# A four-layer graph network: each layer's end as one pipelined block, sums that begin with x in them, small loads and flags beside the sums

## What is computed

```python
x = layernorm(x + L0(x))   # relational: h = relu(segsum(w1 * (x @ W[etype])[src]) + b1); the same again on h, + b2
x = layernorm(x + L1(x))   # graph: h = x @ W; dinv = rsqrt(max(in_deg, 1)); (h + segsum(w * h[src])) * dinv + bias
x = layernorm(x + L2(x))   # attention, 8 heads, twice: softmax over each node's edges, weighted sum; relu between
x = layernorm(x + L3(x))   # tensor product: messages from y[src], edge attributes and an MLP of the edge length
```

## Time and profile before

| what | us |
|---|---|
| median of 3 runs | 9986.03 (9984.52 to 9986.73) |
| the profiled execution's own time | 9983.22 |
| its span, first to last instruction | 9981.5 |
| TensorE busy | 7135.5 (71%) |
| GpSimd busy | 6743.2 (68%) |
| VectorE busy | 6099.3 (61%) |
| ScalarE busy | 3181.8 (32%) |

### The profile page before, as it was taken

How to read it: one execution, slowest core, us unless ns; L and a number is a source line. 1 busy time by engine, 2 the same in 40 slices (tenths; PEclk the granted TensorE clock), 3 DMA queues, 4 the chain that set the end, 5 groups by cost and what they waited for, 6 DMA issues and landing times. The chain is left out here.

```text
span 9981.5 us, 162608 instructions
## 1 busy us (share of the span) xinstructions
PE 7135.5 (71%) x35298; PEld 5014.6 (50%) x35298; DVE 6099.3 (61%) x20565; ACT 3181.8 (32%) x10805; POOL 6743.2 (68%) x7057
## 2 busy tenths in 40 slices
PE   3555554666677666669999857777477777499998
PEld 2222222333333333334444446566366666499998
DVE  8454553444434444446666557777577777699887
ACT  1222220000021000000000045555355555499997
POOL 1777776777734777757777467777377776277775
PEclk9999999999996555555555577877677777699999
DMA  3222222111143111111111122222122222211112
GB/s 89 79 83 84 80 82 78 53 53 53 53 180 136 53 53 53 53 48 53 53 53 53 33 59 60 60 60 60 38 60 60 60 60 52 68 53 52 53 52 45
DMA packets 290879, 638.27 MB, mean 64 GB/s; under 512 B 124766, under 2 KB 160609, under 8 KB 277745
## 3 DMA queue, kind: packets, MB, share of 16 engines
q0 software_dynamic: 224928, 422.56, 16.4%
q1 hardware_dynamic: 65392, 210.05, 6.1%
HBM read 481.27 MB, written 150.87 MB: 63 GB/s over the span
## 5 line engine op out<-in xcount | busy, mean ns | idle before, releaser
L806 POOL DMA_INDIRECT relsum_rows<-relation_table,tab_idx x1994 | 1894.7, 950 | 891.1 <-issue 532.1
L898 PE MATMUL relsum_sums<-relsum_hot,relsum_rows 128*128 128x128 f32 x3988 | 1575.4, 500 | 944.1 <-DMA relsum_rows<-relation_table,tab_idx 665.5
L898 PEld LDWEIGHTS relsum_sums<-relsum_hot,relsum_rows 128*128 128x128 f32 x3988 | 998.4, 312 | 1521.4 <-DMA relsum_rows<-relation_table,tab_idx 1500.6
L806 POOL DMA_INDIRECT conv_rows<-tensor_table,src_idx x1008 | 953.4, 946 | 502.8 <-issue 217.0
L806 POOL DMA_INDIRECT gcnsum_rows<-x_table,src_idx x997 | 945.0, 948 | 366.9 <-issue 231.3
L655 POOL DMA_INDIRECT records<-sort_recs,place_rows x968 | 987.5, 1020 | 295.1 <-issue 295.1
L884 DVE TENSOR_TENSOR rel_acc<-rel_acc,relsum_sums 128x128 f32 x1994 | 574.8, 288 | 992.9 <-PE relsum_sums L898 988.9
L806 POOL DMA_INDIRECT gat2sum_rows<-gat_table,src_idx x1008 | 955.2, 948 | 315.0 <-issue 223.4
L806 POOL DMA_INDIRECT gat1sum_rows<-gat_table,src_idx x1008 | 954.1, 947 | 314.9 <-issue 227.1
L865 DVE TENSOR_SCALAR relsum_hot<-iota_row,dst_rel,w 128x128 f32<-128x128 f32 x1994 | 712.0, 358 | 421.1 <-issue 419.9
L898 PE MATMUL gcnsum_sums<-gcnsum_hot,gcnsum_rows 128*128 128x128 f32 x1994 | 793.9, 502 | 0.0
(11 more groups left out here) (381 smaller groups left out, 14855.3 us busy)
## 6 DMA issues: line engine op xcount, KB each, us to landing
relation_table<-table_row SPq DMA_DIRECT2D x30, 2048.0 KB, 6.3
relation_table<-sort_space SPq DMA_DIRECT2D x40, 1024.0 KB, 5.7
relsum_rows<-relation_table,tab_idx POOLq DMA_INDIRECT x1994, 2.5
place_lo_wide<-lo_rows SPq DMA_DIRECT2D x121, 256.0 KB, 3.5
relation_table<-place_extra SPq DMA_DIRECT2D x20, 1024.0 KB, 5.8
gat1sum_rows<-gat_table,src_idx POOLq DMA_INDIRECT x1008, 2.5
gat2sum_rows<-gat_table,src_idx POOLq DMA_INDIRECT x1008, 2.5
conv_rows<-tensor_table,src_idx POOLq DMA_INDIRECT x1008
```

The source lines that it names most:

```text
L806: pool.indirect_dma_start(bufs[:, t % depth, :], None, table, bass.IndirectOffsetOnAxis(ap=idx[:, t:t + 1], axis=0)).then_inc(landed[t % l ...
L898: pe.matmul(bank[:, 0:P], rows[:, t % depth, :], hot[:, t % HOTS, :], start=True, stop=True).then_inc(s["multiplied"], 1)
```

## The change

- `load_sorted` is gone. `ReloadAndPrepare` runs beside the first relational sum: the records come in 16 pieces into three buffers; GpSimd waits before tile 0, 63, 126, ... for its piece's indices. SyncE then loads the second table's weights and 39 small tensors; TensorE turns x from tile 90 on (a quad of blocks every 4 tiles) and at tile 140 prepares the attention weights; ScalarE writes x turned, with the relational bias added, into the accumulator of the second sum.
- `second_table` gets the weights ready in SBUF and loads only its bias.
- The second relational sum and the graph sum do not clear their accumulator: it begins with x in it. In the graph sum TensorE first turns x (`pe_first`), VectorE then adds the graph bias to x, and only then the tiles start. The flags' groups come every 8 tiles instead of 16, and `crossing_runs` runs at tile 552 to 572.
- `finish_layer` takes the place of `per_node_block`, `normalize`, `project_nodes` and the stores for the first three layers. It works by units of 3 blocks and pairs of units: produce, add to x (or not), statistics, spread, root, shift, normalising by ScalarE, turning, product with the next layer's weights, copy, store of a pair. `finish_tensor_layer` does it for the last one.
- `between_attentions` divides by pairs and goes on with relu, product, copy and store per pair; GpSimd adds the second attention bias to x there.
- `first_scores` has moved into `attend`: its eight gathers are issued ahead of the others.
- Register loops around the nodes' work are unrolled. Three more scopes end with a barrier.

The core of the diff:

```diff
-def load_sorted(env, records):
-            sp.dma_start(rec[:, :, :], records.rearrange("(p q) k -> p q k", p=P)).then_inc(got, 16)
+class ReloadAndPrepare(Beside):
+    def sync(self, sp):
+        for c in range(PIECES):
+            if c >= 3:
+                sp.wait_ge(s["placed"], c - 2)
+                sp.wait_ge(s["weighed"], c - 2)
+            sp.dma_start(self.rec[:, c % 3, :, :], rows[:, c * PIECE:(c + 1) * PIECE, :]).then_inc(self.got[c % 3], 16)
...
+    def pool_at(self, pool, t):
+        if t % PIECE == 0:
+            pool.wait_ge(self.s["indexed"], t // PIECE + 1)
...
+        if t == self.WEIGHTS_AT:
+            pe.wait_ge(s["small_in"], 16 * self.small_loads)
...
+class GraphSum(Beside):
+    def pe_first(self, pe):
+        for q in self.quads():
+            if q:
+                pe.wait_ge(self.s["x_kept"], q)
+            for k, b in enumerate(range(4 * q, min(BLKS, 4 * q + 4))):
+                mm = pe.transpose(self.turn_ps[:, k * P:(k + 1) * P], self.env.x[:, b, :], self.env.ident[:, :])
+            mm.then_inc(self.s["x_turned"], 1)
...
+        dve.wait_ge(s["x_turned"], len(self.quads()))
+        x = self.env.x[:, 0:BLKS, :]
+        dve.tensor_tensor(x, x, over_rows(self.env.gcn_bias[:, :], BLKS), ALU.add)
+        dve.wait_ge(s["x_kept"], len(self.quads()))
...
+def finish_layer(env, tag, how, table=None, weights=None, width=None, scale=None, store_x=None):
+            for u in range(4):
+                make(u)
+            for u in range(UNITS):
+                if weights is not None:
+                    turn_x(u)
+                if u + 4 < UNITS:
+                    make(u + 4)
+                if weights is not None and u:
+                    apply(u - 1)
...
+            for g in range(PAIRS):
+                for u in (2 * g, 2 * g + 1):
+                    dve.wait_ge(s["made"], u + 1)
+                    if how.updates:
+                        how.update(dve, u, made[u % 4]).then_inc(s["freed"], 1)
+                        dve.drain()
+                    for k, b in enumerate(unit_blocks(u)):
+                        dve.bn_stats(env.stats[:, b, :], env.x[:, b, :] if how.updates else made[u % 4][:, k * P:(k + 1) * P])
+                dve.drain()
+                find_spread(dve, env, pair_blocks(g)).then_inc(s["measured"], 1)
+                if how.feeds and g + 2 < PAIRS:
+                    how.feed(dve, g + 2).then_inc(s["fed"], 1)
+                if g:
+                    dve.wait_ge(s["rooted"], g)
+                    find_shift(dve, env, pair_blocks(g - 1)).then_inc(s["shifted"], 1)
...
+            for g in range(PAIRS + 2):
+                if g < PAIRS:
+                    act.wait_ge(s["measured"], g + 1)
+                    act.activation(env.rstd[:, own], env.rstd[:, own], ACT.Sqrt, bias=env.eps[:, 0:1]).then_inc(s["rooted"], 1)
+                if 0 < g <= PAIRS:
+                    norm(g - 1)
...
+def between_attentions(env, acc, table):
+            floor_sums(dve, acc)
+            for g in range(PAIRS):
+                divide_sums(dve, acc, g).then_inc(s["divided"], 1)
...
+            pool.tensor_tensor(x, x, over_rows(env.gat_bias2[:, :], BLKS), ALU.add)
```

More of the change, by code:

```diff
@@ L723, in second_table @@
+def second_table(env, weights, table, hidden, bias):
     nc = env.nc
@@ L924, in per_node_block @@
-        block = ctx.enter_context(nc.Block())
+        made = [ps(f"made{j}", [P, 512], F32) for j in range(4)]
+        turn = [ps(f"turn{j}", [P, 512], F32) for j in range(2)]
+        out = [ps(f"out{j}", [P, 512], F32) for j in range(2)]
+        x_t = sb("x_t", [P, 2, UNIT * P], F32)
+        rows = sb("rows", [P, BLKS, width], F32) if weights is not None else None
+        how.memory(sb, ps, out[1])
+        s = {n: env.sig(f"{tag}_{n}").sem for n in (
+            "fed", "made", "freed", "measured", "rooted", "shifted", "normed", "turned", "kept", "applied", "taken",
+            "taken_dve", "stored")}
@@ L1066, in load_columns, with norm @@
-def load_columns(env, tag, pairs):
-    sig = env.sig("small_loaded")
-    with env.nc.Block() as block:
+            def norm(g):
+                act.wait_ge(s["shifted"], g + 1)
+                for u in (2 * g, 2 * g + 1):
+                    for k, b in enumerate(unit_blocks(u)):
+                        frm = env.x[:, b, :] if how.updates else made[u % 4][:, k * P:(k + 1) * P]
+                        last = act.activation(env.x[:, b, :], frm, ACT.Identity, bias=env.shift[:, b:b + 1],
+                                              scale=env.rstd[:, b:b + 1])
+                    last.then_inc(s["normed"], 1)
@@ L1566, in _ @@
             pe.sem_inc(s["turned"], PHASES)
+            pe.wait_ge(firsts["spread"].sem, firsts["spread"].at(1))
+            for j in range(FIRSTS):
+                mm = pe.matmul(firsts_ps[:, j * HEADS:(j + 1) * HEADS], first_wide[:, j, :, :].rearrange("p k h -> p (k h)"),
+                               env.head_mask[:, :], start=True, stop=True)
+            mm.then_inc(firsts["turned"].sem, 1)
             turn_scores(0, 0)
@@ L1602, in attend, with divide_sums, floor_sums @@
             landed[k].passed(16 * (GRPS // PHASES))
-def divide_sums(env, acc):
-    with env.nc.Block() as block:
+        for n, count in (("gathered", 16 * FIRSTS), ("spread", 1), ("turned", 1)):
+            firsts[n].passed(count)
+def divide_sums(dve, acc, pair):
+    cols = slice(2 * pair * UNIT * P, 2 * (pair + 1) * UNIT * P)
+    dve.reciprocal(acc[:, 1, cols], acc[:, 1, cols])
+    dve.drain()
+    return dve.tensor_tensor(acc[:, 0, cols], acc[:, 0, cols], acc[:, 1, cols], ALU.mult)
+def floor_sums(dve, acc):
+    dve.tensor_scalar(acc[:, 1, 0:NPAD], acc[:, 1, 0:NPAD], 1e-30, None, ALU.max)
+    dve.drain()
@@ new lines, in between_attentions @@
+def between_attentions(env, acc, table):
+    nc = env.nc
+    width = TABLE_WIDTH
+    pair_cols = 2 * UNIT * P
+    with ExitStack() as ctx:
+        sb, ps = stage_memory(nc, ctx, "between")
+        hidden = sb("hidden", [P, 2, pair_cols], F32)
+        rows = sb("rows", [P, BLKS, width], F32)
+        out = [ps(f"out{j}", [P, 512], F32) for j in range(4)]
+        s = {n: env.sig(f"between_{n}").sem for n in ("divided", "hidden", "applied", "taken", "stored")}
+        block = ctx.enter_context(nc.Block())
@@ new lines, in _ @@
+        @block.tensor
+        def _(pe):
+            for u in range(UNITS):
+                pe.wait_ge(s["hidden"], u // 2 + 1)
+                if u >= 4:
+                    pe.wait_ge(s["taken"], u - 3)
+                for k in range(UNIT):
+                    at = (u % 2 * UNIT + k) * P
+                    mm = pe.matmul(out[u % 4][:, k * width:(k + 1) * width], hidden[:, u // 2 % 2, at:at + P], env.gat_w[1][:, :],
+                                   start=True, stop=True)
+                mm.then_inc(s["applied"], 1)
@@ new lines, in finish_tensor_layer, with pair_blocks @@
+        sb, ps = stage_memory(nc, ctx, "tpout")
+        made = [ps(f"made{j}", [P, 512], F32) for j in range(4)]
+        turn = [ps(f"turn{j}", [P, 512], F32) for j in range(2)]
+        x_t = sb("x_t", [P, 4, UNIT * P], F32)
+        s = {n: env.sig(f"tpout_{n}").sem for n in ("turned", "kept", "made", "freed", "measured", "rooted", "shifted", "normed", "stored")}
+        block = ctx.enter_context(nc.Block())
+        def pair_blocks(g):
+            return slice(2 * g * UNIT, 2 * (g + 1) * UNIT)
```

1160 lines of the change are left out of this document (640 added, 520 removed).

## The result

The changed kernel takes 9755.95 us (median of 4 runs, 9751.77 to 9762.47) where the kernel before takes 9985.28 (4 runs, 9984.35 to 9986.73): a ratio of 0.9771, 95% interval 0.9754 to 0.9788. The profiled execution took 9753.1 us for a span of 9751.4, 230.1 us less than that of before. I had said 9759 and 227.2.

The account below looks back on a forecast made before the run. Gains were expected only at stage borders, 529 us where GpSimd has no gather to issue. Terms summed to 227.2 us off the profiled 9983.2, leaving 9756.0; with 2.8 for the median, 9759, range 9728 to 9802.

Parts of the forecast that it names:

- graph end: Border after the graph sum: 133.1 us to 60.1, gain 73.0 (60 to 80), VectorE slowest at 5.5 a pair.
- relational end: Border after the second relational sum: 55.2 us become 36.5, gain 18.7, bounds 8 and 24.
- graph sum's start: First gather to first tile of the graph sum: 23.9 us instead of 10.7, cost 13.2 (9 to 20).
- last end: Border after the convolution, to the kernel's end: 59.7 us become 47.0, gain 12.7 (8 to 16).
- attention end: Border between second attention and convolution: 129.0 us become 71.7, gain 57.3 (47 to 65).
- Records, second table: Reading before the first sum: gain 32.3 us (28 to 34); second table loading only its bias: 8.3 (5 to 9).
- Rival 3: Work beside the first relational sum isn't hidden: 20 to 60 us more, about 9800; chance 0.05.
- The ring: Relational end: a PSUM bank is free only once ScalarE has normalised it, so each pair takes 6.4 us.
- It is TensorE that sets this stage: its 1250 us start later: Graph sum: TensorE bounds it, so its later first tile delays the whole stage, cost 13.2 us.
- rival 1: Graph sum: the dense transposes at its start bring TensorE 2.4 GHz; 21 us less, 9738; chance 0.12.
- rival 2: Graph, attention and last ends: pipelines don't overlap, ScalarE's norms and hand-offs add 37 us, 9796; chance 0.17.
- Between: Border between the two attentions: 93.2 us become 55.1, gain 38.1 (28 to 42 if VectorE and GpSimd collide).

Follow-up runs that it names:

- the late folding: Changed kernel with the two flag-folding matmuls at tiles 976 and 984 instead of 560 and 568: 9753.08 us against 9752.79 (slower chip: 11429.56 against 11430.54).
- pairs first: Changed kernel with TensorE making the next pair's units before turning, VectorE's shift earlier, ScalarE normalising before the next root: 9719.45 us against 9752.79.
- The pieces: Changed kernel with GpSimd's add between the attentions cut into five, each beside a reciprocal: 9743.66 us against 9752.79.
- the second group: Runs on another chip than the slow first one; the changed kernel, unaltered, as yardstick there: 9752.79 us.

## Why the prediction was right, and where it was not

The forecast took the borders between stages, each wholly on the path, and sized what stays of each. That held nearly everywhere: but for the 3.6 us of the graph end's entry (below) no border's gain was lost elsewhere, and the long stages kept their time. Of the eight terms with bounds four lay within them; better than theirs were the relational end (25.1, bound 24), the graph sum's start (7.6 lost, bound 9) and the last end (17.0, bound 16), worse the attention end (46.4, bound 47). (By these same bounds the worst and the best sum are 164 and 261 us, which gives 9822 and 9725, not the 9814 and 9713 of the prediction.) Step by step:

*Records, second table.* As said. 16.2 us from the last scatter, 8.3 for the table, and 8.2 between the last gather's end and the request for the bias as before. Rival 3 is out.

*Relational end: a size.* The ring is 5.1 us a pair, not 6.4 (6 statistics in 1.3, six norms in 2.2, six turns in 2.0), and 30.0 in all.

*Graph sum: the step failed.* "It is TensorE that sets this stage: its 1250 us start later" did not hold: TensorE and the gathers are so close that a late start of TensorE can be made good within the stage. The late start (18.3 us, not 23.9: a quad takes 1.8, not 2.3) cost nothing at the sum's end, since the folding matmuls, which the change moves from the graph end into the sum, raise the clock for 31 us:

```profile
5047.59 0.80 PE L1097 MATMUL gcnsum_sums<-gcnsum_hot,gcnsum_rows 128*128 128x128 f32 x2
5048.31 1.88 PE L1408 MATMUL gcnsum_x_turn<-gcnsum_by_tile,head_sel 128*8 128x512 f32 x2
5049.98 0.63 PE L1096 MATMUL gcnsum_sums<-gcnsum_hot,ones 128*1 128x128 f32 x2
...
5052.26 0.38 PE L1096 MATMUL gcnsum_sums<-gcnsum_hot,ones 128*1 128x128 f32 x2
5052.57 0.49 PE L1097 MATMUL gcnsum_sums<-gcnsum_hot,gcnsum_rows 128*128 128x128 f32 x2
```

A matmul of 0.80 takes 0.49, a tile 0.73 instead of 1.24, and 17 us of lag become 4. From the first gather to the end 1261.6 us pass, and 1262.7 in the kernel before: of my cost of 13.2 nothing is left there. Up to the next stage's first matmul it is 1265.3 against 1263.0, so 2.3 us are, since that matmul now waits for GpSimd's end of the block. The rise is not the only way in which the lag goes: with the late folding it came at tile 976 and the next stage began as soon behind the last gather. That is rival 1 in part. Its sign was right, its trigger was not the dense start but something I had listed under the graph end and costed there alone. Against it the gathers have become slower, 1256.0 us from first to last instead of 1247.6, from 4393.17 to the kernel before's last:

```profile
5640.77 0.95 POOL L806 DMA_INDIRECT gcnsum_rows<-x_table,src_idx  x1 [0.30 <-issue]
```

The idle time between two gathers is the same (0.30 us), the gathers themselves are longer: the one that begins under VectorE's bias row is held up, and so is, a little, one at each group of flags.

```profile
4334.68 0.94 POOL L1054 DMA_INDIRECT gcnsum_rows<-x_table,src_idx  x1 [0.30 <-issue]
4335.93 3.88 POOL L1054 DMA_INDIRECT gcnsum_rows<-x_table,src_idx  x1 [0.30 <-issue]
...
4410.19 1.09 POOL L1054 DMA_INDIRECT gcnsum_rows<-x_table,src_idx  x1 [0.30 <-issue]
```

```profile
4334.83 4.16 DVE L1394 TENSOR_TENSOR x<-x,gcn_bias 128x3840 f32<-128x3840 f32 x1 [6.59 <-PE gcnsum_x_turn L1367]
...
4410.10 0.42 DVE L1422 TENSOR_TENSOR_SCAN flags_lead<-flags_reset 128x127 bf16<-128x127 bf16 x1
```

2.9 us for the first and 0.14 for each of some 65 at the flags, 9.3 together. The kernel before has flags too: there 50 gathers are 0.08 longer, 4.0 together. The difference, 2.9 + 9.3 - 4.0, is the 8.4 but for 0.2. "The flags' transposes cost TensorE the same" was true and beside the point.

*Graph end: 62.6, not 73.0.* By the steps: transposes of the degree 3.4, not 6.7; entry 3.6, which I had at nothing, since the sum now ends 5 us behind the last gather and GpSimd's 8 us at a block's end no longer lie beside TensorE's lag; VectorE's five pairs 32.8, not 28.5; from the last shift to the first gather 19.1, not 13.9; first gathers 10.0, as said. The pairs first:

```profile
5604.36 0.87 DVE L1471 SCALAR_TENSOR_TENSOR x<-gcnout_made,gcnout_dinv,x 128x128 f32<-128x128 f32 x3 [3.57 <-PE gcnout_made L1466]
5611.39 0.87 DVE L1471 SCALAR_TENSOR_TENSOR x<-gcnout_made,gcnout_dinv,x 128x128 f32<-128x128 f32 x3 [2.61 <-PE gcnout_made L1466]
5618.60 0.87 DVE L1471 SCALAR_TENSOR_TENSOR x<-gcnout_made,gcnout_dinv,x 128x128 f32<-128x128 f32 x3 [2.61 <-PE gcnout_made L1466]
```

VectorE is not "the slowest in the pipeline". Its own work is 4.3 us a pair, less than my 5.5, but it waits for TensorE, whose make stands in its queue behind a turn, which waits for ScalarE's norm, which waits for VectorE's shift: 10.4 us in all. That is rival 2's mechanism, in another queue than I looked at; pairs first took it away and with it 15 us. The tail: the last two shifts come together, so ScalarE has two pairs to normalise, where I counted one (2.4 us and its copies), and turns and products ran at 1.2 GHz there, where I had taken 0.93 over.

*Attention end: 46.4, not 57.3.* The same order: waits of 2.93 three times, 1.24 and 0.76, with ScalarE's norm 5.9 us late, since the shift stood behind the division. VectorE's stretch was 61.7 instead of 54.7, and entry and tail 20.9 instead of 17. Pairs first gave 12.6 back.

*Between: 33.0, not 38.1.* The one named bound that came true: the floor took 10.27 us beside GpSimd's add instead of 2.16, 8.1 lost; the rest of the border was 3 us shorter than I said. The pieces brought 8.3 back.

*Last end: a size.* TensorE's part took 30.8 us, not 36.5. I had misread it: in the kernel before it was 35.2 (9921.83 to 9957.04), not 37. Of the 4.4 that the change saves, some 3.1 are the order of work: three blocks are turned at once, and a block takes 1.00 us instead of 1.10. The other 1.3 I put down to the clock: it stayed at 1.00 until beyond TensorE's last matmul, where in the kernel before it was at 0.50 for the first 3.4 us of this end. Four later profiles with the same code here had such a fall at the start too, and their last ends took 43.9 to 44.1 us, where all the others with this code took 42.6 or 42.7. What decides whether it falls is not shown. The rest of the end took 11.9 us, not 10.5.

So the total was right for the wrong shares, by luck: in three borders I said 26.4 us too much, elsewhere some 29 too little. Two mechanisms that I had at their own chances (rivals 1 and 2) both occurred, each in part, with opposite signs.

## What to carry to other kernels

In a pipeline over several engines write down the order of each engine's queue and follow every wait: an operation that could run now but stands behind one that waits for a later step closes a ring over three engines, and no sum of busy times shows it. Whatever can run ahead goes ahead of what waits, and a small result that another engine needs goes ahead of a long operation. And where a stage's bound is close (two engines within 1%), a cost on one of them says little: read how far the later engine is behind the earlier one at the start and at the end of the stage, and what the next stage's first instruction waits for.

## What the runs showed of the hardware

A matmul of 512 columns, once, raised TensorE's clock in a stage that had kept it at 0.50 with TensorE busy throughout; moved, the rise moved with it, on both chips where that was tried. The Trainium skill, "TensorE: Matmul & The Clock Gate", section "What's actually happening", says that activity releases the throttled state: the runs agree behind these matmuls, and not on the 660 us before them, with TensorE busy all the time. Which of their traits does it (the width, the 8 columns of weights) was not tried.

The clock that a profile shows can be wrong, so read it beside the lengths of the matmuls. In the first sum over the relation table, where the code is the same, it stands at 1.00 in some profiles and at 0.50 in others. Here the changed kernel in the second group, then pairs first:

```profile
1600.00:2800.00 1200.00, 763.18 (x1996) 494.63 (x1996) 526.88 (x1993) 12.74 (x38) 907.45 (x961) 1.00 0.23 60
```

```profile
1600.00:2800.00 1200.00, 763.90 (x1996) 494.73 (x1996) 527.84 (x1995) 12.74 (x38) 907.45 (x960) 0.50 0.23 60
```

The same 1996 matmuls keep TensorE busy for 763.2 and 763.9 us, and in the profile with 1.00 a tile's product takes 0.80 us, as it does in the graph sum at 0.50, and not 0.49 as behind the folding matmuls:

```profile
2699.61 0.80 PE L1097 MATMUL relsum_sums<-relsum_hot,relsum_rows 128*128 128x128 f32 x2 [0.45 <-DVE rel_acc L1082]
```

So TensorE was equally slow in both, and the sum took the same time (1245.6 and 1245.3 us). The mean clock of a whole execution, 0.79 or 0.73 for the same kernel, differs by as much as this one stretch makes (half of 1242 us), so it says nothing on the speed. In the graph sum the clock shown and the lengths of the matmuls agree.

GpSimd's drain at the end of a block is over 8.0 us after the last of 997 gathers (2851.9 and 5649.7 in the kernel before, 5587.2 in the changed one), and 1.9 to 2.0 us after the last of eight. And a chip can be 17% slower on the same program (11637 against 9985 us) with its gathers at their usual 948 ns.
